# Wide attention in a four-layer transformer kernel: values issued in pairs every second tick, and the extras of a batch spread anew

## The chip, the cores and the metric

The kernel runs on one core of a Trainium2 chip. The metric is the device time of one execution in microseconds; the median of several runs is compared.

## The reference, cut to what matters

The model has four layers on a state x of 16 sequences of 256 positions and 128 channels. The change is in the attention of layers 0 and 1, the "wide" one: 16 heads of 64 channels. (h is the normed and modulated x.)

```python
# layer 0: causal, with normed and rotated q and k
q, k, v = split(h @ wqkv.T)            # 16 heads of 64
q, k = rope(rmsnorm(q, wq)), rope(rmsnorm(k, wk))
attn = softmax(where(causal, q @ k.T * 64 ** -0.5, -inf))
x = x + ga * ((attn @ v) @ wo.T)
# layer 1: a bias by relative position, no mask
scores = q @ k.T * 64 ** -0.5 + bias
x = x + ga * ((softmax(scores) @ v) @ o_w.T)
```

## The kernel before, in words

The whole program is one list of stages. Each engine runs them in the same order, and semaphores join the engines. `wide_attention` (line 414) makes two of the stages: the causal one (layer 0, some 40 to 660 us of the profile) and the biased one (layer 1, some 1050 to 1645 us).

**Ticks.** A batch is one of the 16 sequences. Its 16 heads make eight pairs, p = 8 b + j, and the stage's loop has one tick t per pair (lines 696, 870, 965, 1036). With u = t % 8, tick t also does 1/8 of the projections of a later batch a and prepares batch b = t // 8 + 1. What each engine does in a tick, and in which order, is written out by hand:

- TensorE (lines 696 to 709): `tensor_project`, in the causal stage `tensor_turn` (the rotated q and k transposed), `tensor_sums` (line 579, the transpose of the reciprocal sums, line 584), `tensor_extra` (line 586: V projection, output product c0 or c1, transposes of the norm), then scores of t, transposes of the probabilities of t-1 (line 643), and the value product of t-2 (`value`, line 653).
- VectorE (lines 870 to 887): copies or rotation products of the projection, `vector_spread` (copy of the turned sums, line 752), `vector_extra`, row maxima and their negation (`rowmax`, or `biased_rowmax`, line 809, with the negation in line 822), the reciprocal (line 762), the even half of the transposed probabilities of t-1 out of PSUM into TS (line 884), sums of squares.
- ScalarE (lines 965 to 984): copies, `scalar_extra`, the odd half of the transposed probabilities of t-1, the four exponentials of t (`exps`, line 934), and in odd ticks the copy of a finished pair of values from bank 4 into OT (line 982).
- GpSimd (`gpsimd_tick`, line 1002): in the causal stage K's scaling (line 1012), the rotation's additions (991, 992) and a power (1000); in both the scaling of OT by the reciprocal sums (line 1026) and the residual.
- SP: one round trip of the reciprocal sums through memory per batch (lines 1047 to 1058).

**Banks.** PSUM has eight banks. Pair p has banks 2 (p % 2) and the next for scores and, after the exponentials, for its transposes. So the scores of t+1 wait until both halves of the transposes of t-1 have been copied out (line 616), and VectorE makes its half after the maxima of t. Bank 4 takes the values of two pairs. Banks 5 to 7 are a ring: projection, q and k turned, V, sums' transpose, output product and norm transposes take its banks in turn, in the order of `take_tick` (line 495).

**Where the extras of a batch stand.** V's four parts at u = 2, 3, 4, 5 (`v_at`; parts 0 and 2 are copied by VectorE, 1 and 3 by ScalarE); the sums: reciprocal at u=0, transpose at 1, scalings at 3 and 4, output products at 6 and 7 (`posts`, line 472); the norm's transposes at 0, every second batch (`turned_in`, line 483).

**Buffers.** TS, the transposed probabilities, has two buffers. WM (768 columns) and CT hold the weights of the layer's modulation; WF has 6400 columns, of which the biased stage uses 6144.

## Time and profile before

| | us |
|---|---|
| median of 3 runs (2927.63 to 2938.03) | 2928.72 |
| profiled execution | 2927.48 |
| its span | 2924.9 |
| TensorE busy | 2768.8 (95%) |
| VectorE busy | 2120.6 (73%) |
| ScalarE busy | 1700.9 (58%) |
| GpSimd busy | 1043.8 (36%) |
| mean granted TensorE clock | 0.987 of full |

The span goes from the first to the last instruction; 2.6 us of the profiled execution's own time lie around it. Busy time is a union over an engine's instructions. A matmul's end is modelled, so starts are the better measure: the time from one set of probability transposes (line 643) to the next is a tick. One fp32 product is two records in the trace.

### The profile page before, as it was taken

To read this page: it belongs to the slowest core of one execution; us is meant where nothing else is said; L and a number is where in the kernel's file an instruction comes from. 1 tells how busy PE (TensorE), PEld (TensorE's weight loads), DVE (VectorE), ACT (ScalarE), POOL (GpSimd) and SP (SyncE) were. 2 spreads that over 40 slices of the span, in tenths; PEclk is the share of its full clock that TensorE was granted. 3 is DMA by queue.
4 is the path that set the end of the run, shared out by engine and by line. 5 is a ranking of instruction groups with operands and counts; after the bars stand their busy time and mean duration, and the time that the engine had idled before them with its cause. 6 is when DMAs were issued, how large, how long until landed. Compare 5 with 4: busy or idle time off the path is not lost.

```text
span 2924.9 us, 68989 instructions
## 1 busy us (share of the span) xinstructions
PE 2768.8 (95%) x25484; PEld 1867.5 (64%) x25484; DVE 2120.6 (73%) x5801; ACT 1700.9 (58%) x4109; POOL 1043.8 (36%) x1422
## 2 busy tenths in 40 slices
PE   5999999989999999999999799999989988999898
PEld 2666666666666666666666455567767765666676
DVE  6988888855666566666666699855678886887675
ACT  3888888873332367777776477644325544343665
POOL 6888888831000011111111345412243330104441
PEclk9999999999999999999999899999999999999999
DMA  3111111123000011111111554300026443245760
GB/s 106 23 24 31 31 31 31 31 74 102 1 15 1 1 36 31 31 31 30 24 26 28 144 158 131 102 1 16 1 80 174 124 120 79 59 103 131 192 178 26
DMA packets 191996, 186.96 MB, mean 64 GB/s; under 512 B 14528, under 2 KB 168192, under 8 KB 190896
## 3 DMA queue, kind: packets, MB, share of 16 engines
q1 hardware_dynamic: 191664, 182.56, 24.5%
q8 instruction: 205, 3.36, 0.5%
q14 instruction: 127, 1.04, 0.1%
HBM read 129.19 MB, written 53.31 MB: 62 GB/s over the span
## 4 chain that ended last, share of the span: by engine, by line
PE 75%; DVE 10%; ACT 6%; issue 3%; POOL 2%; DMA 2%; SPq 2%; ACTq 0%; DVEq 0%; POOLq 0%
PE pb L161 67%; ACT big L947 4%; PE pb L643 3%; ACT big L158 2%; DVE big L2198 2%; DVE big L817 1%; PE pb L576 1%; SPq L1869 1%; PE pb L2169 1%; DVE big L2699 1%; DMA big<-parts 1%; PE pb L246 1%; DVE big L233 1%; POOL big L1026 1%; DVE big L727 0%
## 5 line engine op out<-in xcount | busy, mean ns | idle before, releaser
L161 PE MATMUL pb<-big 64*128 64x256 bf16 (+12 forms) x20300 | 2509.7, 329 | 92.3 <-DVE big L2198 32.0
L161 PEld LDWEIGHTS pb<-big 128*128 128x128 f32 (+5 forms) x20300 | 1565.9, 145 | 834.6 <-issue 502.3
L158 ACT ACTIVATE big<-pb 128x512 f32<-128x512 f32 (+7 forms) x1444 | 828.5, 623 | 542.0 <-PE pb L161 308.1
L158 ACT ACTIVATE big<-pb,big 128x512 f32<-128x512 f32 (+2 forms) x536 | 316.0, 617 | 541.4 <-PE pb L161 476.8
L2198 DVE TENSOR_REDUCE big<-pb 128x4 f32<-128x1024 f32 (+1 forms) x256 | 277.6, 1086 | 75.6 <-PE pb L161 71.0
L172 POOL TENSOR_TENSOR big<-big 128x128 f32<-128x128 f32 x192 | 84.8, 456 | 649.3 <-DVE big L169 649.3
L947 ACT ACTIVATE big<-big 128x256 f32<-128x256 f32 x512 | 253.9, 498 | 69.8 <-DVE big L822 68.7
L947 ACT ACTIVATE big<-pb,big 128x128 f32<-128x128 f32 (+1 forms) x512 | 256.9, 525 | 61.1 <-DVE big L802 60.9
L817 DVE CUSTOM_DVE_ANT_0 big<-pb,big 128x256 f32<-128x256 f32 x512 | 186.6, 421 | 100.2 <-PE pb L161 100.2
L1543 DVE SCALAR_TENSOR_TENSOR big<-pb,big 128x128 f32<-128x128 f32 x512 | 144.0, 344 | 138.3 <-PE pb L161 137.5
L1026 POOL TENSOR_TENSOR big<-big 128x512 f32<-128x512 f32 x128 | 159.9, 1276 | 233.8 <-DMA big<-recip 233.7
L1521 DVE SCALAR_TENSOR_TENSOR big<-pb,big 128x512 f32<-128x512 f32 x200 | 148.5, 749 | 89.8 <-PE pb L161 60.6
L185 POOL TENSOR_SCALAR big<-big 128x4 f32<-128x4 f32 (+2 forms) x105 | 27.3, 260 | 495.2 <-DVE big L180 495.2
L643 PEld LDWEIGHTS pb<-big 64*128 64x128 f32 x3584 | 145.8, 139 | 74.9 <-ACT big L947 58.0
L643 PE MATMUL pb<-big 64*128 64x64 f32 x3584 | 158.0, 225 | 25.5 <-ACT big L947 24.6
L1000 POOL TENSOR_TENSOR big<-big 128x32 f32<-128x32 f32 x32 | 174.1, 5441 | 2.7
L727 DVE TENSOR_TENSOR big<-pb,big 128x512 f32<-128x512 f32 x256 | 163.7, 680 | 13.2 <-PE pb L161 11.4
L884 DVE COPY big<-pb 128x384 f32<-128x384 f32 (+1 forms) x256 | 156.8, 612 | 2.3 <-PE pb L643 2.1
L991 POOL TENSOR_TENSOR big<-big 128x256 f32<-128x256 f32 x128 | 83.7, 654 | 84.3 <-DVE big L727 81.1
L576 PEld LDWEIGHTS pb<-big 128*128 128x128 f32 x512 | 63.7, 142 | 75.9 <-issue 65.6
L947 ACT ACTIVATION_READ_ACCUMULATOR big<-pb,big 128x1 f32 x512 | 110.6, 216 | 0.0
L233 DVE TENSOR_SCALAR big<-big 128x128 f32<-128x128 f32 x256 | 97.5, 433 | 8.0 <-POOL big L187 7.9
(147 smaller groups left out, 2193.8 us busy)
## 6 DMA issues: line engine op xcount, KB each, us to landing
big<-parts SPq DMA_DIRECT2D x96, 512.0 KB, 4.2
parts<-big SPq DMA_DIRECT2D x384, 96.0 KB, 2.4
big<-recip SPq DMA_DIRECT2D x64, 512.0 KB, 6.6
big<-comb SPq DMA_DIRECT2D x32, 512.0 KB, 8.2
parts<-big SPq DMA_DIRECT2D x192, 64.0 KB, 2.1
big<-gates SPq DMA_DIRECT2D x7, 1024.0 KB, 6.1
big<-in_wf SPq DMA_DIRECT2D x1, 3072.0 KB, 14.7
big<-scratch SPq DMA_DIRECT2D x1, 3072.0 KB, 17.4
```

Of the source, the lines that this page charges most:

```text
L158: return e.activation(o, i, f, bias=bias, scale=scale)
L161: return e.matmul(o, l, r_, start=start, stop=stop, skip_group_check=True)
L643: t = e.transpose(banks[2 * (p % 2) + half][:, 64 * at:64 * at + 64], PS[p % 2][rows, i, 128 * blk:128 * blk + 128], IDF[rows, rows])
L727: t = e.tensor_tensor(h3(D), h3(bk), TAB[:, 2 * qk + kk, tile, :].unsqueeze(1).to_broadcast([128, 8, 64]), ALU.mult)
L817: t = e.tensor_tensor_reduce(ps[:, i, x], banks[2 * (p % 2) + i][:, x], U[:, 2 * j + i, 128 - 128 * qt:384 - 128 * qt], 1.0, -3.0e38, ALU. ...
L884: e.tensor_copy(*turned_out(t - 1, 0)).then_inc(even_out, 1)
L947: t = e.activation(ps, banks[2 * s + i][:, at:at + w] if causal else ps, ACT.Exp, bias=NM[s][:, m:m + 1], scale=rstd_q(b)[:, qt, h:h + 1] ...
L1000: e.tensor_tensor(half, half, HALF, ALU.pow).then_inc(rms_made, 1)
L1026: e.tensor_tensor(OT[k % 6], OT[k % 6], R[:, 2 * i:2 * i + 2, :], ALU.mult).then_inc(chunk_scaled, 1)
L1521: e.scalar_tensor_tensor(out=H[n % hn], in0=bk[:, :], scalar=B2[:, nf * u + f:nf * u + f + 1], in1=sg, op0=ALU.add, op1=ALU.mult).then_inc ...
L1543: x = e.scalar_tensor_tensor(out=ACC[s][:, i, :], in0=bk[:, 128 * i:128 * i + 128], scalar=CMB[s][:, E * i + u:E * i + u + 1], in1=ACC[s][ ...
L2198: e.tensor_reduce(m[:, :, 0:n, jj], two[:, :, 0:width].rearrange("p e (q x) -> p e q x", q=n), AXX, ALU.max, negate=True).then_inc(maxed, 1)
```

## The change

1. `value` is no longer called once a tick but twice in odd ticks, for pairs t-3 and t-2. The stage has 131 ticks in place of 130.
2. TS gets a third buffer: WM's columns in the causal stage, in the biased one 1024 columns made of WF's unused 256 and WM. The loads of the modulation's weights for layer 2 (CT and WM) move from the start of the biased stage to the narrow attention stage after it.
3. V's parts move to u = 3, 4, 5 and u = 0 of the batch after; the wait for V's copies goes from the scores of a batch's first pair to its first value. The sums' transpose moves from u=1 to 2, the scalings from 3 and 4 to 4 and 5, the norm's transposes from 0 to 1. Reciprocal (0) and output products (6, 7) stay.
4. In the biased stage the maxima are negated and announced per head of the pair, two negations of 2 columns in place of one of 4; `exps` goes head by head and waits for the second head's maxima only before its third exponential. In the causal stage the exponentials keep their order.
5. On GpSimd the scaling of OT comes first in its tick, ahead of K's scaling, additions, powers and norm.

```diff
@@ -111,6 +111,7 @@
         WF = alloc(6400)
+        spare_at = top[0] - 256
         WM = alloc(768)
@@ -435,7 +436,7 @@
             width = 384 if causal else 512
-            TS = [alloc(2 * width) for _ in range(2)]
+            TS = [alloc(2 * width) for _ in range(2)] + [WM if causal else big[:, spare_at:spare_at + 1024]]
             OT = [alloc(512).rearrange("p (j t) -> p j t", j=2) for _ in range(6)]
@@ -460,10 +461,15 @@
             hosted = not causal
-            last = 128 + 2
+            last = 128 + 3
             guests_at = 120 if causal else 112
             ahead = 2 if causal else 1
-            v_at = (2, 3, 4, 5)
+            def values_in(b, u):
+                found = (b - 1, 3) if u == 0 else (b, u - 3) if u in (3, 4, 5) else None
+                return [found] if found and 0 <= found[0] < 16 else []
@@ -471,7 +477,7 @@
-                return [(step, t // 8 - 1) for step, late in (("recip", 0), ("turn", 1), ("scale0", 3), ("scale1", 4), ("c0", 6), ("c1", 7))
+                return [(step, t // 8 - 1) for step, late in (("recip", 0), ("turn", 2), ("scale0", 4), ("scale1", 5), ("c0", 6), ("c1", 7))
                         if t >= 8 and t % 8 == late]
@@ -484,7 +490,7 @@
                     return (a + 1) // 2 if u == 7 else None
-                return (a + 1) // 2 if a < 15 and a % 2 == 1 and u == 0 else None
+                return (a + 1) // 2 if a < 15 and a % 2 == 1 and u == 1 else None
@@ -501,8 +507,8 @@
                         take(step, c, ring=ring)
-                if 0 <= b < 16 and u in v_at:
-                    take("v", b, v_at.index(u), ring=ring)
+                for v in values_in(b, u):
+                    take("v", *v, ring=ring)
                 for step, c in posts(t):
@@ -584,8 +590,8 @@
             def tensor_extra(e, t, a, b, u):
-                if 0 <= b < 16 and u in v_at:
-                    tensor_v(e, b, v_at.index(u))
+                for v in values_in(b, u):
+                    tensor_v(e, *v)
                 for step, c in posts(t):
@@ -609,7 +615,7 @@
                 if j == 0:
-                    for key in (("v", b, 2), ("v", b, 3)) + ((("turn", b, 7),) if causal else (("project", b, 6), ("project", b, 7))):
+                    for key in (("turn", b, 7),) if causal else (("project", b, 6), ("project", b, 7)):
                         s = slots[key]
@@ -647,11 +653,15 @@
                 n = width // 64
-                return (TS[p % 2].rearrange("p (n q) -> p n q", n=n)[:, :, 64 * half:64 * half + 64],
+                return (TS[p % 3].rearrange("p (n q) -> p n q", n=n)[:, :, 64 * half:64 * half + 64],
                         banks[2 * (p % 2) + half][:, 0:width].rearrange("p (n q) -> p n q", n=n))
...
                 b, j, c = p // 8, p % 8, p // 2
+                if j == 0:
+                    for n in (2, 3):
+                        s = slots["v", b, n]
+                        e.wait_ge(s.free, s.n)
                 e.wait_ge(even_out, p0 + p + 1)
@@ -661,7 +671,7 @@
                         t = mm(e, o[64 * i:64 * i + 64, 256 * (p % 2) + q0:256 * (p % 2) + 256], VB[b % 2][:, kb, 2 * j + i, :],
-                               TS[p % 2][:, width * i + 256 * kb:width * i + 256 * kb + 256 - q0], kb == 0, kb == 1)
+                               TS[p % 3][:, width * i + 256 * kb:width * i + 256 * kb + 256 - q0], kb == 0, kb == 1)
                 t.then_inc(pair_valued, 1)
@@ -703,7 +713,8 @@
                         turn(e, t - 1)
-                    if 0 <= t - 2 < 128:
+                    if t >= 3 and t % 2:
+                        value(e, t - 3)
                         value(e, t - 2)
@@ -770,8 +781,9 @@
                         residual_vector(e, r0 + qt, qt, bk[:, 0:128], 0).then_inc(s.free, 1)
-                if 0 <= b < 16 and u in v_at[0::2]:
-                    vector_v(e, b, v_at.index(u))
+                for v in values_in(b, u):
+                    if v[1] % 2 == 0:
+                        vector_v(e, *v)
                 c = normed_in(a)
@@ -816,14 +828,14 @@
                                                    U[:, 2 * j + i, 128 - 128 * qt:384 - 128 * qt], 1.0, -3.0e38, ALU.add, ALU.max,
-                                                   nm[:, 2 * qt + i:2 * qt + i + 1])
-                t.then_inc(own_v.sem, own_v.up())
-                e.wait_ge(own_v.sem, own_v.n)
-                e.tensor_scalar(nm, nm, -1.0, None, ALU.mult).then_inc(pair_maxed, 1)
+                                                   nm[:, 2 * i + qt:2 * i + qt + 1])
+                    t.then_inc(own_v.sem, own_v.up())
+                    e.wait_ge(own_v.sem, own_v.n)
+                    e.tensor_scalar(nm[:, 2 * i:2 * i + 2], nm[:, 2 * i:2 * i + 2], -1.0, None, ALU.mult).then_inc(pair_maxed, 1)
             def ts_writable(e, p):
-                if p >= 2:
-                    e.wait_ge(pair_valued, p0 + p - 1)
+                if p >= 3:
+                    e.wait_ge(pair_valued, p0 + p - 2)
@@ -885,6 +897,7 @@
                         guest.vector(e, t - guests_at)
+                e.wait_ge(pair_valued, p0 + 128)
@@ -920,8 +933,9 @@
             def scalar_extra(e, a, b, u):
-                if 0 <= b < 16 and u in v_at[1::2]:
-                    scalar_v(e, b, v_at.index(u))
+                for v in values_in(b, u):
+                    if v[1] % 2:
+                        scalar_v(e, *v)
                 c = turned_in(a, u)
@@ -932,21 +946,23 @@
             def exps(e, p):
                 s, b, j = p % 2, p // 8, p % 8
-                e.wait_ge(pair_maxed, p0 + p + 1)
+                e.wait_ge(pair_maxed, p0 + (p + 1 if causal else 2 * p + 1))
                 if p >= 2:
...
                     e.wait_ge(recip_made, b0 + b - 1)
-                for qt in range(2):
+                for n in range(4):
+                    qt, i = (n // 2, n % 2) if causal else (n % 2, n // 2)
                     at = 0 if qt == 0 else width - 256
                     w = 128 if causal and qt == 0 else 256
-                    for i in range(2):
-                        ps = PS[s][:, i, at:at + w]
-                        m, h = 2 * qt + i, 2 * j + i
-                        t = e.activation(ps, banks[2 * s + i][:, at:at + w] if causal else ps, ACT.Exp, bias=NM[s][:, m:m + 1],
-                                         scale=rstd_q(b)[:, qt, h:h + 1] if causal else 1.0,
-                                         accum_out=SM[b % 2][:, 2 * h + qt:2 * h + qt + 1])
+                    if n == 2 and not causal:
+                        e.wait_ge(pair_maxed, p0 + 2 * p + 2)
+                    ps, h = PS[s][:, i, at:at + w], 2 * j + i
+                    t = e.activation(ps, banks[2 * s + i][:, at:at + w] if causal else ps, ACT.Exp, bias=NM[s][:, n:n + 1],
+                                     scale=rstd_q(b)[:, qt, h:h + 1] if causal else 1.0,
+                                     accum_out=SM[b % 2][:, 2 * h + qt:2 * h + qt + 1])
                 t.then_inc(pair_exped, 1)
@@ -1000,6 +1016,14 @@
             def gpsimd_tick(e, t, a, b, u):
+                for step, c in posts(t):
+                    if step in ("scale0", "scale1"):
+                        half = int(step[5])
+                        e.wait_ge(ld_recip, 32 * (b0 + c + 1))
+                        for i in (2 * half, 2 * half + 1):
+                            k = 4 * c + i
+                            e.wait_ge(chunk_out, c0 + k + 1)
+                            e.tensor_tensor(OT[k % 6], OT[k % 6], R[:, 2 * i:2 * i + 2, :], ALU.mult).then_inc(chunk_scaled, 1)
                 if causal and 0 <= b < 16:
@@ -1017,14 +1041,7 @@
                 for step, c in posts(t):
-                    if step in ("scale0", "scale1"):
-                        half = int(step[5])
-                        e.wait_ge(ld_recip, 32 * (b0 + c + 1))
-                        for i in (2 * half, 2 * half + 1):
-                            k = 4 * c + i
-                            e.wait_ge(chunk_out, c0 + k + 1)
-                            e.tensor_tensor(OT[k % 6], OT[k % 6], R[:, 2 * i:2 * i + 2, :], ALU.mult).then_inc(chunk_scaled, 1)
-                    elif step in ("c0", "c1"):
+                    if step in ("c0", "c1"):
                         qt = 2 * c + int(step[1])
@@ -1042,8 +1059,6 @@
                     second_gates(e, 1)
-                    e.dma_start(CT, dr["c2"]).then_inc(ld_wm, 16)
-                    e.dma_start(WM, dr["wmod2"]).then_inc(ld_wm, 16)
                 for b in range(16):
@@ -1073,7 +1088,7 @@
                           lambda e, i: hosted_step(i, lambda *at: gpsimd_tick(e, *at)), nothing)
-            left = (3, 4, 6, 7)
+            left = (4, 5, 6, 7)
             tail = Guest(4, lambda i: take_tick(128 + left[i], 16, 17, left[i], ring=BK[6:8]),
@@ -2444,6 +2459,8 @@
                         e.dma_start(WA[:, 1152:2176], dr["rope8"]).then_inc(ld_wa, 16)
+                        e.dma_start(CT, dr["c2"]).then_inc(ld_wm, 16)
+                        e.dma_start(WM, dr["wmod2"]).then_inc(ld_wm, 16)
                     if k == 2 and b == 5:
```

## Rows read from the trace of the kernel before

**Rows 1.** Busy us of each engine (x instructions) by stretch, TensorE clock, DMA.

```profile
100.00:560.00 460.00, 453.79 (x4247) 299.02 (x4241) 403.66 (x822) 379.83 (x1164) 389.36 (x380) 1.00 0.15 31
1080.00:1535.00 455.00, 448.28 (x4017) 311.47 (x4015) 309.26 (x1207) 323.42 (x1058) 76.83 (x82) 1.00 0.15 30
```

**Rows 2.** Line 584 in those stretches, TensorE; first and last start.

```profile
L584 PE MATMUL pb<-big x13: 272/273/285, 101.8 to 553.2; 128*32 128x128 f32 x13
...
L584 PE MATMUL pb<-big x13: 272/272/273, 1081.0 to 1530.7; 128*32 128x128 f32 x13
```

**Rows 3.** Timeline, TensorE, biased stage; start, us, engine, line, what, count, idle.

```profile
1306.24 0.66 PE L643 MATMUL pb<-big 64*128 64x64 f32 x16
1306.83 4.07 PE L161 MATMUL pb<-big 128*64 128x256 f32 x22
1310.74 0.66 PE L643 MATMUL pb<-big 64*128 64x64 f32 x16
...
1325.53 5.00 PE L161 MATMUL pb<-big 128*64 128x256 f32 x36
```

**Rows 4.** Timeline, TensorE, narrow windows inside one tick of the biased stage.

```profile
1307.10 0.60 PE L161 MATMUL pb<-big 128*64 128x256 f32 x4
...
1307.32 0.39 PE L161 MATMUL pb<-big 128*64 128x256 f32 x2
...
1307.85 0.48 PE L161 MATMUL pb<-big 128*128 128x256 f32 x1
...
1308.82 0.59 PE L161 MATMUL pb<-big 128*128 128x512 f32 x1
...
1309.77 0.49 PE L161 MATMUL pb<-big 64*128 64x256 f32 x2
```

**Rows 5.** Timeline, TensorE, transposes of the first two biased ticks.

```profile
1049.59 0.71 PE L643 MATMUL pb<-big 64*128 64x64 f32 x16 [1.91 <-ACT big L947]
...
1053.13 0.66 PE L643 MATMUL pb<-big 64*128 64x64 f32 x16
```

**Rows 6.** Timeline, VectorE, biased stage, two ticks.

```profile
1303.89 0.35 DVE L762 RECIPROCAL big<-big 128x32 f32<-128x32 f32 x1
...
1306.46 0.42 DVE L817 CUSTOM_DVE_ANT_0 big<-pb,big 128x256 f32<-128x256 f32 x1 [0.24 <-PE pb L161]
...
1306.81 0.42 DVE L817 CUSTOM_DVE_ANT_0 big<-pb,big 128x256 f32<-128x256 f32 x1
...
1308.04 0.69 DVE L884 COPY big<-pb 128x512 f32<-128x512 f32 x1
```

**Rows 7.** Timeline, biased stage: sums' transpose, scalings, a negation.

```profile
1305.07 0.27 PE L584 MATMUL pb<-big 128*32 128x128 f32 x1
...
1315.69 4.97 POOL L1026 TENSOR_TENSOR big<-big 128x512 f32<-128x512 f32 x4 [12.20 <-DMA big<-recip]
...
1316.94 1.28 DVE L822 TENSOR_SCALAR big<-big 128x4 f32<-128x4 f32 x1
```

**Rows 8.** Timeline, TensorE, causal stage (PEld: its weight loads).

```profile
252.21 0.27 PE L584 MATMUL pb<-big 128*32 128x128 f32 x1
...
263.16 0.53 PE L643 MATMUL pb<-big 64*128 64x64 f32 x12
...
267.66 0.53 PE L643 MATMUL pb<-big 64*128 64x64 f32 x12
...
274.92 2.93 PE L161 MATMUL pb<-big 128*128 128x128 f32 x28
...
283.12 0.53 PE L643 MATMUL pb<-big 64*128 64x64 f32 x12
...
287.04 0.45 PEld L643 LDWEIGHTS pb<-big 64*128 64x128 f32 x12 [0.51 <-ACT big L947]
```

**Rows 9.** Timeline, GpSimd, causal stage.

```profile
263.88 2.51 POOL L1026 TENSOR_TENSOR big<-big 128x512 f32<-128x512 f32 x2
...
268.74 2.50 POOL L1026 TENSOR_TENSOR big<-big 128x512 f32<-128x512 f32 x2
```

## The prediction, made before the change was run

> **What bounds the kernel now.** The page comes first: its busy line and its slices show TensorE at nine tenths nearly everywhere, at a full clock, in the two stages that the diff touches. The busy time by stretch then sets those stages side by side [rows 1]: in the 460 us of the causal stage TensorE is busy 453.79 us, with VectorE at 403.66, GpSimd at 389.36 and ScalarE at 379.83 close behind; in the 455 us of the biased stage TensorE has 448.28 and VectorE only 309.26, GpSimd 76.83. So TensorE sets the pace, but in the causal stage three engines run little below it. The line of the sums' transpose, once a batch of eight ticks, gives the period [rows 2]: (553.2 - 101.8) / 12 = 37.62 us in the causal stage, (1530.7 - 1081.0) / 12 = 37.47 us in the biased one. Each stage has about 14 regular batches and two at its end.
>
> Next, one tick of the biased stage on TensorE, from the start of one set of probability transposes to the next: 1310.74 - 1306.24 = 4.50 us, no idle time [rows 3]. Its parts [rows 3, 4]: transposes 0.59, values 1.02 (1306.83 to 1307.85), projection 0.97, V projection 0.95, scores 0.97. A pass over two head halves takes 0.22 (1307.10 to 1307.32), so four passes of a value need 0.86 to 0.88 and the rest of the 1.02 is spent on entering and leaving that tile shape. The first ticks of the stage have no value yet and show what a tick without one costs [rows 5]: 1053.13 - 1049.59 = 3.54 us with V, 0.96 less. A causal tick with V and a value is 267.66 - 263.16 = 4.50 too [rows 8]; its second key block is half as wide, so I put its value at 0.96 - 0.22 = 0.74, and the second value of a pair at 0.65.
>
> Work of TensorE alone for a biased batch: eight ticks without V at 4.50 - 0.95 = 3.55, 28.4; four V, 3.8; two output products, each 5.00 - 4.07 + 0.95 = 1.88 above a plain tick [rows 3], 3.76; sums' transpose 0.2; norm transposes every second batch, 0.3. That is 36.4, so about 1.1 us of 37.47 is stall. In the causal batch V needs no change of tile shape, which I take as 0.1 less, 0.86; the rest is put alike: 8 x 3.64 + 4 x 0.86 + 3.6 + 0.4 = 36.6 of 37.62, 1.0 of stall.
>
> **Values in pairs.** A pair costs 0.96 + 0.86 = 1.82 in place of 2 x 0.96, so 0.10 less per two ticks, 0.4 per batch, in either stage. The third TS buffer makes this possible without a wait: at tick t the copy writes the buffer whose value was issued a tick earlier. What it does to the order matters more. An even tick now has no value: from scores of t to scores of t+1 TensorE has only transposes, projection, an extra and scores, 0.59 + 0.97 + 0.97 = 2.53 us plus the extra; the odd tick has 4.4 plus its extra. The extras sit at these places: even-to-odd intervals get norm transposes (u=1, half the batches), V (3), V (5), output product (7); the longer ones get V (0), sums (2), V (4), output product (6).
>
> **What is late next, biased stage.** Scores of t+1 need the bank that VectorE empties after it has finished the maxima of t. From the transposes' start at 1306.24 VectorE begins the maxima 0.22 later and reaches the copy at 1308.04, 1.80 later [rows 6]; the copy takes 0.69, end +2.49. The change negates each head's maxima by itself, in program order ahead of this copy. A maximum takes 1306.81 - 1306.46 = 0.35, so four of them leave 1308.04 - 1306.46 - 1.40 = 0.2 for wait and negation, and a second negation adds about as much: +2.70, with 0.05 for the semaphore (an estimate) +2.75. Then 0.97 of scores: an even-to-odd interval is at least 3.72 us. TensorE's own work for it is 2.55 without an extra, 2.85 as a mean over batches with and without a norm, 3.5 with V, 4.4 with an output product. Stalls: u=1, 3.72 + 0.27 (the reciprocal stands between negation and copy, 0.35 long, of which I put 0.27 as not overlapped) - 2.85 = 1.1; u=3, 0.2; u=5, 0.2; u=7 none. The exponentials are not this bound: with the first head's maxima ready two passes, 0.7 us, earlier they can start sooner. That part of the change is a gain on a chain that stops being last.
>
> **The negations and GpSimd.** In the tick of the trace where GpSimd begins its four scalings (1315.69, 4.97 us), VectorE's negation takes 1.28 us instead of 0.17, from 1316.94 to 1318.22, beside GpSimd's second one, which ends near it [rows 7]. The tick then waits for the exponentials. The change gives each tick two such negations and moves the scalings one tick later; they arrive 10.6 us after the sums' transpose (1315.69 against 1305.07), which lands in u=4, an even tick. First negation: 0.3 late; second: 0.5; so 0.75 more at u=5. Bounds: nothing if the scalings miss it, as much as 1.28 x 2 if both wait a whole scaling; I take 0.75. The Trainium skill (SBUF — State Buffer, section "SBUF: two separate sides") says of a port pair shared by VectorE and GpSimd that whoever starts first holds it for a whole instruction and the other fully blocks. The trace agrees with it, 1.28 against 0.17; were the long negation a chance of something else, the biased batch would come out 0.75 shorter, about 37.5.
>
> Biased sum: 36.4 - 0.4 + 1.1 + 0.2 + 0.2 + 0.75 = 38.25, against 37.47: +0.8 per batch, x14 = +11 us.
>
> **Causal stage.** Here the exponentials keep their order. With a long extra ahead of it, the interval 283.12 to 287.04 is 3.92 us and was ended by ScalarE [rows 8]: the chain scores, maxima, exponentials, transposes. Even-to-odd intervals of 2.9 + extra (3.76 with V) hit it at u=1 (stall 0.8), 3 and 5 (0.16 each). The present stalls of u=0 and 1 (3.92 against 3.64 at u=0, and at u=1 a tick made long by statistics or modulation) lie in the long intervals afterwards and go. Without more: 36.6 - 0.4 + 1.1 = 37.3, a gain of 0.3.
>
> Against it stands the moved sums' transpose. It goes from u=1 to u=2, the output product stays at u=6. Now: transpose 252.21, scalings from 263.88, last pair 268.74 to 271.24, product 274.92 [rows 8, 9]; the scalings end 19.0 after the transpose, 3.7 before the product, which is due 22.7 after it. The changed order takes out of this one interval of 4.5 and the stall of tick 1 (0.7 by the sum above), turns three of 4.5 into 3.92, 5.15 and 3.92 (-0.5) and adds a second value (+0.65): due at 17.65. The scalings will stand ahead of K's scaling and the additions of their tick, but a K scaling and an addition still lie between the two pairs, as now: 268.74 - 263.88 - 2.51 = 2.35, and 7.4 from first to end. The data land at +10.6 in the biased stage, where GpSimd waits for them idle [rows 7]; I put it at +10.85 here, with a slower copy ahead, so the end is at 10.85 + 7.4 = 18.25 and TensorE waits 0.6 us. Bounds: nothing if the data land by 10.25, 1.9 where one more GpSimd scaling's length (2.51 / 2) lies in the way. I take 0.85, nearer to the row. Causal sum: 37.3 + 0.85 = 38.15 against 37.62: +0.55, x14 = +8 us. In the biased stage GpSimd has nothing between the pairs, the scalings end at 15.6, 2 us before the product.
>
> **The ends and the loads.** In the last, emptier ticks the even ticks are stall-bound sooner: about +1 us per stage. The sums' transpose of the last batch goes behind two values in place of one, 0.7 to 1.0 us each time, on the chain that ends with the last scalings. Together +4. The two loads for the next modulation move into the narrow stage's SP queue: two issues among many, nothing on a chain, bounds 0 and 1.2.
>
> Sum: 11 + 8 + 4 = +23 on the profiled execution of 2927.5, so 2950.5; the median of the runs shown is 1.2 higher, 2951.7. I say 2951.
>
> **Rivals.** (1) No measurable change: the two tolls (0.75 at u=5, 0.85 at the causal product) are missed or halved. The batches are then 37.5 and 37.3 to 37.7, with the ends +4: 2928 to 2940. For it: each toll hangs on less than one us of alignment. Against: nothing removes the 3.72 of VectorE. (2) Faster: VectorE's copy doesn't gate the short intervals (its work slides into the long ones) and TensorE alone decides: 36.0 and 36.2 per batch, -1.45 x 28 = -41 us, 2888; the half of it, 2905 to 2910, if only the stalls that now stand at u=0, 1 and 4 go. For it: the biased stage has VectorE idle a third of the time. Against: the wait is one of order, not of load. (3) A dearer slow case: in the causal stage VectorE, at 88% busy, can't follow intervals of 3.9 with V on it at u=3 and 5, and comes late into the even tick: 0.6 more per causal batch and the whole second bound of the scalings, 1.05 more: x14 = 23, 2974. (4) That the change is empty can't be: the order of values differs in 126 ticks of each stage; it is part of (1).
>
> **Chances.** Forecast (2940 to 2963) 0.45; no change 0.26; faster 0.22; dearer 0.07. A measurement of this kernel can tell about 0.5%, 14.6 us, from no change; 2914 to 2943 is "same". Faster 0.22, same 0.27, slower 0.51. Range 2902 to 2968: it leaves out the best half of the faster case and the top of the dearer one. The forecast's own range is 2940 to 2963.
>
> **What would show it.** Right: transposes to transposes alternating about 3.7 to 3.9 and 5.3 us; idle time of TensorE ahead of scores in odd ticks, released by the VectorE copy (now hardly any); twice as many negations, some over 0.4 us, near the scalings; idle time before the first product of each causal batch, released by the GpSimd scaling; periods of the sums' transpose above 38. Wrong: a period below 37.3 in either stage, or short intervals of 3.5 with V and no idle time.

## The result, and the profile after

The changed kernel takes 2952.64 us (median of 4 runs, 2951.91 to 2956.15) against 2931.28 us for the kernel before (4 runs, 2927.63 to 2938.03): a ratio of 1.0075, 95% interval 1.0057 to 1.0093. It is slower by 21 us. Forecast were 2951 us and +23, with 2940 to 2963 as the forecast's own range. The profiled execution took 2951.91 us, its span is 2950.0, 25.1 above the span of before.

The busy line of the page: TensorE does the same 25484 matmuls and is busy for 25.5 us less. Of this 19.6 are the pairs' (2762.9 us are busy in the experiment e1 below, which differs in them alone); what makes up the rest was not taken apart.

```profile
PE 2743.3 (93%) x25484; PEld 1875.7 (64%) x25484; DVE 2129.2 (72%) x5929; ACT 1702.0 (58%) x4109; POOL 1042.0 (35%) x1422
```

The busy time by stretch of the changed kernel, to be read beside [rows 1]. In the same 455 us of the biased stage TensorE now has 3904 records, not 4017, and is busy 425.90 us, not 448.28: it waits 29.1 us in place of 6.7.

```profile
100.00:560.00 460.00, 442.26 (x4211) 297.95 (x4211) 393.76 (x817) 381.22 (x1155) 384.23 (x373) 1.00 0.15 29
1080.00:1535.00 455.00, 425.90 (x3904) 308.86 (x3902) 309.97 (x1277) 313.83 (x1035) 77.10 (x82) 1.00 0.14 30
```

The sums' transpose (now line 590) in the same stretches, once a batch. The periods are (524.1 - 106.3) / 11 = 37.98 us in the causal stage and (1514.2 - 1091.4) / 11 = 38.44 us in the biased one, against 37.62 and 37.47 [rows 2].

```profile
L590 PE MATMUL pb<-big x12: 272/273/273, 106.3 to 524.1; 128*32 128x128 f32 x12
...
L590 PE MATMUL pb<-big x12: 272/273/273, 1091.4 to 1514.2; 128*32 128x128 f32 x12
```

One biased batch on TensorE from the timeline (line 649 is the transposes of the probabilities, so the distance between two of its rows is a tick; the last bracket gives the idle time ahead of a row and what ended it):

```profile
1361.48 0.66 PE L649 MATMUL pb<-big 64*128 64x64 f32 x16
...
1364.21 1.14 PE L162 MATMUL pb<-big 64*128 64x256 f32 x8 [0.15 <-DVE big L896]
1365.18 0.66 PE L649 MATMUL pb<-big 64*128 64x64 f32 x16
...
1370.54 0.66 PE L649 MATMUL pb<-big 64*128 64x64 f32 x16
...
1374.38 1.14 PE L162 MATMUL pb<-big 64*128 64x256 f32 x8 [1.27 <-DVE big L896]
1375.35 0.66 PE L649 MATMUL pb<-big 64*128 64x64 f32 x16
...
1381.64 0.66 PE L649 MATMUL pb<-big 64*128 64x64 f32 x16
...
1386.04 0.66 PE L649 MATMUL pb<-big 64*128 64x64 f32 x16
...
1391.40 0.66 PE L649 MATMUL pb<-big 64*128 64x64 f32 x16
...
1394.34 1.13 PE L162 MATMUL pb<-big 64*128 64x256 f32 x8 [1.22 <-DVE big L896]
1395.31 0.66 PE L649 MATMUL pb<-big 64*128 64x64 f32 x16
```

Short and long ticks alternate: 3.70 (1361.48 to 1365.18), 5.36, 4.81, 6.29, 4.40, 5.36, 3.91. The short ticks with V (3.70 and 4.81) and the one of the reciprocal (3.91) have idle time in front of the scores, and each is ended by line 896, VectorE's copy. In the whole stretch TensorE's matmuls (PE) wait 29.0 us for this copy, which is nearly all of their 29.1 us of idle time. The weight loads (PEld) wait 52.8, but they overlap the matmuls, so the two rows are not to be added:

```profile
PEld pb L162 <- DVE big L896: 52.8, 36, 2.3
PE pb L162 <- DVE big L896: 29.0, 35, 1.5
```

In the kernel before, no matmul of this stretch waits for the copy (line 884 there). Some weight loads do, and the matmuls' idle time is ended by the exponentials:

```profile
PEld pb L161 <- DVE big L884: 15.6, 24, 1.0
...
PE pb L643 <- ACT big L947: 6.2, 20, 0.4
```

Why the third tick is 4.81 and not 3.7 can be read from GpSimd's and VectorE's timelines. GpSimd's four scalings:

```profile
1369.97 4.97 POOL L1026 TENSOR_TENSOR big<-big 128x512 f32<-128x512 f32 x4 [22.41 <-DMA big<-recip]
```

VectorE's two negations of that tick, the copy behind them, and one negation of the next tick for comparison:

```profile
1371.56 0.94 DVE L834 TENSOR_SCALAR big<-big 128x2 f32<-128x2 f32 x1
...
1373.22 0.52 DVE L834 TENSOR_SCALAR big<-big 128x2 f32<-128x2 f32 x1
1373.65 0.68 DVE L896 COPY big<-pb 128x512 f32<-128x512 f32 x1
...
1376.38 0.17 DVE L834 TENSOR_SCALAR big<-big 128x2 f32<-128x2 f32 x1
```

The first negation takes 0.94 us and ends at 1372.50, the second 0.52 and ends at 1373.74, both at the end of a scaling (four in 4.97 us: 1371.2, 1372.5, 1373.7); undisturbed it is 0.17. This is no single case: of the 256 negations of the stage 32 take more than 0.3 us, and 30 of these end within 0.03 us of the end of a scaling.

Mean time from transposes to transposes over 13 regular batches (second to fourteenth of each stage), from the starts of line 643 or 649, by the u of the tick at its end; the forecast's row is made of its own terms:

| | u=0 | 1 | 2 | 3 | 4 | 5 | 6 | 7 | sum |
|---|---|---|---|---|---|---|---|---|---|
| biased, before | 4.06 | 4.05 | 4.52 | 4.49 | 4.84 | 4.59 | 5.42 | 5.42 | 37.4 |
| biased, forecast | 5.35 | 3.99 | 4.61 | 3.72 | 5.35 | 4.47 | 6.28 | 4.46 | 38.2 |
| biased, after | 5.36 | 3.91 | 4.61 | 3.70 | 5.36 | 4.82 | 6.28 | 4.40 | 38.4 |
| causal, before | 4.00 | 4.43 | 4.56 | 4.51 | 4.52 | 4.65 | 5.49 | 5.43 | 37.6 |
| causal, forecast | 5.15 | 3.92 | 4.50 | 3.92 | 5.15 | 3.92 | 6.95 | 4.70 | 38.2 |
| causal, after | 5.16 | 3.67 | 4.47 | 4.27 | 5.16 | 4.26 | 6.26 | 4.63 | 37.9 |

The causal stage hides something of its own. GpSimd's scalings, VectorE's product of the maxima (line 814, a 128x4 tensor product in SBUF) beside them, and the projection of tick 5 in another batch:

```profile
192.76 2.50 POOL L1026 TENSOR_TENSOR big<-big 128x512 f32<-128x512 f32 x2 [4.40 <-DMA big<-recip]
...
197.43 2.53 POOL L1026 TENSOR_TENSOR big<-big 128x512 f32<-128x512 f32 x2
```

```profile
193.43 0.68 DVE L812 TENSOR_REDUCE big<-pb 128x2 f32<-128x512 f32 x1
194.14 1.14 DVE L814 TENSOR_TENSOR big<-big 128x4 f32<-128x4 f32 x1
```

```profile
230.77 0.53 PE L649 MATMUL pb<-big 64*128 64x64 f32 x12
231.75 1.13 PE L162 MATMUL pb<-big 128*128 128x512 f32 x2 [0.46 <-ACT big L159]
```

The product takes 1.14 us where it mostly takes 0.16, and ends when a scaling does. And the projection starts 0.98 after the transposes, where it starts 0.46 after them in a tick without such a wait (235.46 after 235.00). ScalarE ended that wait; in the code it is ScalarE's square that frees the ring bank which the projection takes. Over the 13 regular batches the projection of tick 3 waits so in every one, 0.5 us on average, that of tick 5 in three. Neither was in the forecast. What was in it, matmuls of the product at u=6 waiting for GpSimd's scalings, comes to little in the 460 us:

```profile
PE pb L162 <- POOL big L1026: 0.4, 2, 0.2
```

### The profile page after: what moved, and what is told of

It reads as the page before. It is cut to its first block, busy times and chain, and to the rows that moved or that the text cites. A ratio compares the mean times of both kernels' runs of the same rounds, so it can differ in the third digit from the quotient of the medians.

```text
span 2950.0 us, 69113 instructions
## 1 busy us (share of the span) xinstructions
PE 2743.3 (93%) x25484; PEld 1875.7 (64%) x25484; DVE 2129.2 (72%) x5929; ACT 1702.0 (58%) x4109; POOL 1042.0 (35%) x1422
## 3 DMA queue, kind: packets, MB, share of 16 engines
q14 instruction: 128, 1.05, 0.1%
## 4 chain that ended last, share of the span: by engine, by line
PE 70%; DVE 13%; issue 5%; ACT 4%; POOL 4%; DMA 2%; SPq 1%; DVEq 0%; ACTq 0%; POOLq 0%
PE pb L162 64%; DVE big L829 2%; ACT big L963 2%; PE pb L649 2%; ACT big L159 2%; DVE big L2213 2%; SPq L1884 1%; POOL big L1026 1%; DVE big L896 1%; PE pb L2184 1%; DVE big L738 1%; DVE big L2716 1%; PE pb L582 1%; DVE big L812 1%; POOL big L1016 1%
## 5 line engine op out<-in xcount | busy, mean ns | idle before, releaser
L162 PE MATMUL pb<-big 128*128 128x128 f32 (+12 forms) x20300 | 2491.0, 329 | 151.5 <-DVE big L896 51.2
L829 DVE CUSTOM_DVE_ANT_0 big<-pb,big 128x256 f32<-128x256 f32 x512 | 196.0, 421 | 134.5 <-PE pb L162 134.4
L963 ACT ACTIVATION_READ_ACCUMULATOR big<-pb,big 128x1 f32 x512 | 103.5, 202 | 0.0
L234 DVE TENSOR_SCALAR big<-big 128x128 f32<-128x128 f32 x256 | 91.5, 411 | 8.4 <-POOL big L188 8.2
```

The source lines that it names most:

```text
L162: return e.matmul(o, l, r_, start=start, stop=stop, skip_group_check=True)
L829: t = e.tensor_tensor_reduce(ps[:, i, x], banks[2 * (p % 2) + i][:, x], U[:, 2 * j + i, 128 - 128 * qt:384 - 128 * qt], 1.0, -3.0e38, ALU. ...
L963: t = e.activation(ps, banks[2 * s + i][:, at:at + w] if causal else ps, ACT.Exp, bias=NM[s][:, n:n + 1], scale=rstd_q(b)[:, qt, h:h + 1] ...
```

## The experiments

All of them keep the whole computation but one (short scalings). In the cuts of code, `...` stands for lines left out. Times are medians against runs of the kernel before on the same chip, with the 95% interval of the ratio; periods come from the sums' transpose, as above.

**One value a tick** (e1_each_tick), the pairs alone undone.

```diff
-                    if t >= 3 and t % 2:
-                        value(e, t - 3)
+                    if 0 <= t - 2 < 128:
                         value(e, t - 2)
```

> The changed kernel, but one value a tick as before; places of the extras, third buffer and split negation kept. Theory (short even ticks are what costs): no interval is held at 3.7 any more, ticks are 4.5 with V; biased period about 37.4 or less (36.4 of TensorE + 0.3 at u=1 + 0.7 where GpSimd holds the negations) against 38.44, causal about 37.3 against 37.98; total 2925 to 2935. Rival (the new places of the extras cost, not the pairs): stays at 2950.

Measured: 2927.19 us, 0.9981 (0.9970 to 0.9992).

```profile
L590 PE MATMUL pb<-big x13: 272/273/273, 105.7 to 553.7; 128*32 128x128 f32 x13
...
L590 PE MATMUL pb<-big x13: 272/273/273, 1084.5 to 1528.0; 128*32 128x128 f32 x13
```

Periods (553.7 - 105.7) / 12 = 37.33 and (1528.0 - 1084.5) / 12 = 36.96. Time and periods are as expected or below. The pairs cost 25 us (2952.64 against 2927.19); everything else in the change together is a small gain, 5 us. TensorE's waits for VectorE's copy in the biased stretch fall from 29.0 to 5.7 us. The rival falls.

**Pairs, extras at their old places** (e5_old_places).

```diff
-                found = (b - 1, 3) if u == 0 else (b, u - 3) if u in (3, 4, 5) else None
+                found = (b, u - 2) if u in (2, 3, 4, 5) else None
...
-(("recip", 0), ("turn", 2), ("scale0", 4), ("scale1", 5), ("c0", 6), ("c1", 7))
+(("recip", 0), ("turn", 1), ("scale0", 3), ("scale1", 4), ("c0", 6), ("c1", 7))
...
-                return (a + 1) // 2 if a < 15 and a % 2 == 1 and u == 1 else None
+                return (a + 1) // 2 if a < 15 and a % 2 == 1 and u == 0 else None
...
-            left = (4, 5, 6, 7)
+            left = (3, 4, 6, 7)
```

> The changed kernel with pairs, but the extras back where they were (V at 2 to 5, sums' transpose 1, scalings 3 and 4, norm's transposes 0). Theory: the 3.7 floors stay (u=1, 3, 5), but the scalings fall into the long tick after u=3, so their toll of 1.1 at u=5 goes: biased period 37.5, causal 37.5; total 2933. Rival (the pairs are the whole cost): 2950.

Measured: 2931.89 us, 1.0001 (0.9992 to 1.0011).

```profile
L590 PE MATMUL pb<-big x13: 272/273/285, 101.7 to 555.9; 128*32 128x128 f32 x13
...
L590 PE MATMUL pb<-big x13: 284/285/286, 1079.7 to 1530.2; 128*32 128x128 f32 x13
```

Periods (555.9 - 101.7) / 12 = 37.85 and (1530.2 - 1079.7) / 12 = 37.54. The biased ticks u=1, 3 and 7 stay at 3.91, 3.70 and 4.40, and u=5 comes down to 3.80, as the toll leaves it. As expected, but for the causal stage, which stays at 37.85 and not 37.5. So 20 us hang on where the extras meet the pairs: a batch of short and long ticks has a parity, and the change had put the scalings on the short side. That it is the scalings shows in the regular batches of the biased stage, 0.9 us or 13 us in all: u=5 falls by 1.02 there, while V's and the norm's moves nearly cancel (u=0 5.36 to 4.70, u=2 4.61 to 5.36). In the causal stage the regular batches give 2 us. The rest lies in the last batches of the stages and was not taken apart.

**A single negation** (e3_one_negation); `exps` waits for it once.

```diff
-                    t.then_inc(own_v.sem, own_v.up())
-                    e.wait_ge(own_v.sem, own_v.n)
-                    e.tensor_scalar(nm[:, 2 * i:2 * i + 2], nm[:, 2 * i:2 * i + 2], -1.0, None, ALU.mult).then_inc(pair_maxed, 1)
+                t.then_inc(own_v.sem, own_v.up())
+                e.wait_ge(own_v.sem, own_v.n)
+                e.tensor_scalar(nm, nm, -1.0, None, ALU.mult).then_inc(pair_maxed, 1)
...
-                e.wait_ge(pair_maxed, p0 + (p + 1 if causal else 2 * p + 1))
+                e.wait_ge(pair_maxed, p0 + p + 1)
...
-                    if n == 2 and not causal:
-                        e.wait_ge(pair_maxed, p0 + 2 * p + 2)
```

> The changed kernel with a single negation and one announcement per pair of heads in the biased stage. Theory: the exponentials, 4.05 after the scores, take the place of VectorE's 3.72 as the floor of the even-to-odd intervals: +0.35 at u=3, +0.15 at u=1, about the same at u=5: biased period 38.9 to 39.1, total 2960. Rival (the second negation is itself the toll): period under 38.2, total 2948 or less.

Measured: 2961.94 us, 1.0105 (1.0086 to 1.0125).

```profile
L590 PE MATMUL pb<-big x12: 272/272/273, 1096.4 to 1523.3; 128*32 128x128 f32 x12
```

The period is (1523.3 - 1096.4) / 11 = 38.81, and u=1 and u=3 are both 4.05 us. The time is as expected, the period a little under. The chain of the exponentials is the floor again; the split negation is worth 9 us within the changed kernel. At u=5 the single negation is cheaper, 4.61 against 4.82, so the rival's toll exists but is the smaller part.

**Short scalings** (e4_short_scalings). GpSimd scales 8 of 256 columns; the others stay unscaled, so this kernel's result is not the model's, and only its times count.

```diff
-                            e.tensor_tensor(OT[k % 6], OT[k % 6], R[:, 2 * i:2 * i + 2, :], ALU.mult).then_inc(chunk_scaled, 1)
+                            e.tensor_tensor(OT[k % 6][:, :, 0:8], OT[k % 6][:, :, 0:8], R[:, 2 * i:2 * i + 2, 0:8], ALU.mult).then_inc(chunk_scaled, 1)
```

> The changed kernel with GpSimd's scalings cut to 8 of 256 columns (the rest of OT is left unscaled), in both stages. Theory: negations and products of the maxima are no longer held behind a GpSimd scaling; biased u=5 falls from 4.82 to 3.70 us, causal u=5 from 4.26 to about 3.75: periods 37.3 and 37.5, total 2930. Rival (u=5 is long because of VectorE's own work): u=5 stays above 4.6 in the biased stage, total 2950.

Measured: 2915.67 us, 0.9948 (0.9934 to 0.9962).

```profile
L590 PE MATMUL pb<-big x13: 272/273/273, 106.0 to 555.3; 128*32 128x128 f32 x13
...
L590 PE MATMUL pb<-big x12: 272/273/273, 1113.1 to 1524.4; 128*32 128x128 f32 x12
```

Periods (555.3 - 106.0) / 12 = 37.44 and (1524.4 - 1113.1) / 11 = 37.39. Biased u=5 falls to 3.75, causal u=5 to 3.91 and u=6 to 6.13. The toll in the biased stage is 1.05 us a batch. The time is 37 us under the changed kernel's, 14 more than expected. Of the 38.5 us between the two profiled executions, 14 batches at 1.05 and 0.54 give 22. What I had not counted: the last batches of the two stages give 4; the stretch from the causal stage's last transposes to the biased stage's first is 6 shorter, since the last four scalings, 5 us long, stand in the chain that ends the causal stage; and the stretch behind the biased stage, whose code is the same, was 7 us shorter in this profiled execution.

**The split alone, on the kernel before** (e2_before_split). Its edit is the reverse of e3's together with the changed `exps`.

> The kernel before with one part of the change alone: maxima negated per head and exponentials head by head in the biased stage. Theory: the chain scores to exponentials of 4.05 falls to about 3.4, so u=0 falls to 3.7 and the sums' tick stays near 4; the second negation can be held by GpSimd too, which adds up to 0.5 at u=4. Biased period 36.9 to 37.1 against 37.47, causal unchanged, total 2922 to 2926. Rival (the split only adds an instruction): 2932 or more.

Measured: 2921.91 us, 0.9965 (0.9951 to 0.9979).

```profile
L584 PE MATMUL pb<-big x13: 272/273/273, 1081.7 to 1523.3; 128*32 128x128 f32 x13
```

The period is (1523.3 - 1081.7) / 12 = 36.80, a little better than expected, and the causal one is 37.62 as before. By itself this part of the change is a gain of 9 us. e1, which keeps all of the change but the pairs, gained 5, so the other parts together gained nothing that these runs show.

**ScalarE negates** (e6_pairs_scalar, e7_each_tick_scalar, e9_old_places_scalar). VectorE announces each head's maxima at once; ScalarE makes the negation ahead of that head's exponentials, 0.19 us of work (the cut shows the edit of `exps` alone). e7 puts this on e1, e9 on the old places with one value a tick.

```diff
+                    if n % 2 == 0 and not causal:
+                        if n:
+                            e.wait_ge(pair_maxed, p0 + 2 * p + 2)
+                        e.activation(NM[s][:, n:n + 2], NM[s][:, n:n + 2], ACT.Copy, scale=-1.0).then_inc(own_a.sem, own_a.up())
+                        e.wait_ge(own_a.sem, own_a.n)
```

> The changed kernel, with the negation of the biased stage made by ScalarE ahead of each head's exponentials, none on VectorE. Theory: VectorE's floor falls to 2.3 + 0.97 = 3.3 and no negation can be held by GpSimd; the exponentials take over at about 3.85, so u=1, 3 and 5 come to 3.85: biased period 37.5 to 37.6 against 38.44, total 2940. Rival (u=5 is held by something other than the negation): u=5 stays near 4.8, total 2950.

Measured: 2944.29 us, 1.0048 (1.0031 to 1.0064).

```profile
L591 PE MATMUL pb<-big x12: 272/272/273, 1096.8 to 1511.6; 128*32 128x128 f32 x12
```

The period is (1511.6 - 1096.8) / 11 = 37.71 and the total 4 us over what was expected; u=1, 3 and 5 are 3.84, 3.85 and 3.84, as expected. With no negation on VectorE nothing is held at u=5. Three floors in the same place have now been read: 3.70 by VectorE's copy, 3.85 and 4.05 by the exponentials.

> One value a tick, the changed places, the negation on ScalarE. Theory: u=5 of the biased stage falls from 4.88 to 4.49 and u=1 stays at or under 3.98: biased period 36.5 against 36.96, total 2921. Rival (ScalarE, now with the longer chain, holds short ticks at 3.85 to 4.1): 2927 as without it.

Measured: 2921.59 us, 0.9972 (0.9961 to 0.9982).

```profile
L591 PE MATMUL pb<-big x13: 272/272/273, 105.5 to 555.8; 128*32 128x128 f32 x13
...
L591 PE MATMUL pb<-big x13: 272/273/273, 1087.1 to 1527.4; 128*32 128x128 f32 x13
```

Periods (555.8 - 105.5) / 12 = 37.53 and (1527.4 - 1087.1) / 12 = 36.69; u=5 of the biased stage is 4.49. Total and u=5 are as expected, the period 0.2 over.

> One value a tick, the extras where they were before, third buffer, scalings first in GpSimd's tick, the negation on ScalarE. Theory: the causal product no longer waits for the scalings (5.84 to 5.49 at u=6), but statistics and norm make u=1 long again as before (4.5): causal period 37.4 to 37.6; biased 36.5. Total 2920 to 2925. Rival (the new places are the better ones): more than e7_each_tick_scalar by 5.

Measured: 2927.59 us, 0.9998 (0.9988 to 1.0008).

```profile
L591 PE MATMUL pb<-big x13: 272/273/273, 102.1 to 557.9; 128*32 128x128 f32 x13
...
L591 PE MATMUL pb<-big x13: 272/273/273, 1085.7 to 1530.9; 128*32 128x128 f32 x13
```

A miss, and its rival holds: periods (557.9 - 102.1) / 12 = 37.98 and (1530.9 - 1085.7) / 12 = 37.10, 6 us slower than e7. So without pairs, and with the rest as in e7, the new places are the better ones. It shows at u=1 (biased 3.95 against 4.26, causal 3.97 against 4.44) and at the causal u=5 (4.53 against 4.96). My reading for u=1, that the norm's modulation and the statistics no longer fall on the same tick's chain, is argued from the order and not shown. Nor does it hold for old places as such: e2, with the old places and GpSimd's old order, takes 2921.91 us, as little as e7.

**Scalings at their old place in GpSimd's tick** (e8_scalings_last): the block of the scalings moved back behind K's scaling and the additions.

> The changed kernel with GpSimd's scalings at their old place in its tick, behind K's scaling and the additions. Theory: in the causal stage the first pair starts later only by what GpSimd has not finished when the data land, and the second pair no earlier; the product at u=6 waits up to 1 us more, or a hold at u=5 moves by as much; the biased stage has nothing else on GpSimd and stays at 38.44. Total 2950 to 2965. Rival (scalings first only delay K's scaling): faster, 2945 or less.

Measured: 2955.01 us, 1.0092 (1.0076 to 1.0108).

```profile
L590 PE MATMUL pb<-big x12: 272/273/273, 108.9 to 530.5; 128*32 128x128 f32 x12
```

Within what was expected. The causal period is (530.5 - 108.9) / 11 = 38.33 against 37.98; u=5 is 4.11, but u=6 waits until 6.81 in every batch. The biased stage stays at 38.46. The times alone, 2955.01 and 2952.64 with overlapping intervals, don't tell the two apart; by the causal period the move is a small gain at these places. At the old places no run tests it alone.

**Both scalings in one tick** (e10_scalings_together), on e7.

```diff
-(("recip", 0), ("turn", 2), ("scale0", 4), ("scale1", 5), ("c0", 6), ("c1", 7))
+(("recip", 0), ("turn", 2), ("scale0", 4), ("scale1", 4), ("c0", 6), ("c1", 7))
```

> As e7_each_tick_scalar, with both pairs of scalings in tick 4, K's scaling and additions behind them. Theory: in the causal stage the scalings end 2.4 earlier, so the product at u=6 does not wait (5.94 falls to 5.49) and one product of maxima less is held: causal period 37.0 against 37.53, biased unchanged at 36.7, total 2914 to 2917, under both kernels. Rival (K's scaling, late by 2.4, holds the turned k at u=6 or 7): no gain.

Measured: 2910.61 us, 0.9942 (0.9928 to 0.9956), the fastest of all, under both kernels.

```profile
L591 PE MATMUL pb<-big x13: 272/273/273, 105.4 to 547.7; 128*32 128x128 f32 x13
...
L591 PE MATMUL pb<-big x12: 272/272/273, 1116.2 to 1519.7; 128*32 128x128 f32 x12
```

The causal period is (547.7 - 105.4) / 12 = 36.86; u=6 falls from 5.94 to 5.46, as expected. The second effect, a product of the maxima less held, isn't seen: u=5 is 4.53 and 4.52. The total is 3 us better than the expected range, which no run explains.

**ScalarE's copy of a pair of values later** (e11_late_copy).

```diff
-                    if 0 <= t - 2 < 128 and t % 2 == 1:
-                        c = (t - 2) // 2
-                        e.wait_ge(pair_valued, p0 + t - 1)
+                    if 0 <= t - 3 < 128 and t % 2 == 0:
+                        c = (t - 3) // 2
+                        e.wait_ge(pair_valued, p0 + t - 2)
```

> The changed kernel, but ScalarE copies a finished pair of values out of bank 4 at the end of the even tick instead of the odd one, half a microsecond of work off the way to its squares. Theory (in the causal stage the projection of an odd tick waits for the ring bank that ScalarE's square of the even tick frees): causal u=3 falls from 4.48 to 3.9 or 4.0 where it is long, u=5 falls by up to 0.4, u=1 stays at 3.6 to 3.8: causal period 37.3 to 37.5 against 37.98; the biased stage stays at 38.4; total 2943 to 2948. Rival (these ticks are long by VectorE's work): causal period 37.9 to 38.1, total 2952.

Measured: 2949.08 us, 1.0075 (1.0051 to 1.0100).

```profile
L590 PE MATMUL pb<-big x12: 272/273/273, 107.0 to 524.6; 128*32 128x128 f32 x12
```

The waits view of the causal stretch, the changed kernel first, then this one:

```profile
PE pb L162 <- ACT big L159: 7.7, 15, 0.7
...
PE pb L162 <- ACT big L159: 3.6, 12, 0.4
```

A miss: the period is the rival's. The ticks moved the way of the theory, if by less (u=3 from 4.27 to 4.09, u=5 from 4.26 to 4.11), but the causal period is (524.6 - 107.0) / 11 = 37.96, unchanged: what they gave, u=2 (4.47 to 4.62) and u=6 (6.26 to 6.43) took. In those of its batches whose u=5 is short, 3.70 to 3.76, u=6 is 6.6; where it is long, 4.4 to 4.7, u=6 is 6.2. The product's wait for the scalings stands behind whatever wait comes before it. That the bank's wait alone makes u=3 long is thus supported, not settled.

## Why the prediction was right, point by point

- **TensorE alone sets the pace before.** Right. With one value a tick the biased period reaches 36.96 (e1) and 36.69 (e7), near the 36.4 that was summed for TensorE's own work, and the causal one 36.86 (e10), near its 36.6.
- **A pair saves 0.10.** Right in kind, short in size. The unhindered long ticks are 5.36 and 5.16, forecast 5.35 and 5.15, but the short one with the output product is 4.40 and not 4.46. Two ticks with a product took 5.42 + 5.42 before and take 6.28 + 4.40 now, 0.16 less. Over 128 pairs this is 20 us, which is what TensorE's busy time gained (19.6 against e1). The forecast had taken a single value as 0.96, from the stage's first ticks, and not as the 1.02 of its own rows.
- **VectorE's copy behind two negations is the floor, 3.72 us.** Right, 3.70, and 3.91 with the reciprocal (3.99). It is idle time ahead of the scores, ended by line 896. Without negations on VectorE (e6) the exponentials' 3.85 stands in its place; without short ticks (e1) the waits fall from 29.0 to 5.7 us. The point was one of order: VectorE is busy 309.97 of 455 us and still ends these waits.
- **The chain of the exponentials becomes harmless.** Right; without the split it is 4.05 (e3).
- **The toll of the scalings at u=5, 0.75.** The mechanism was right, the size short: 1.1 (4.82 against 3.70, and e4's 3.75). The two negations were put at 0.3 and 0.5 late; in the row they are 0.77 and 0.35. The scalings come 9.66 after the sums' transpose (1369.97 against the 1360.31 of line 590), not 10.6: VectorE, idle here, copies the sums 0.3 after the transpose, not 0.9. The rule of the Trainium skill that the prediction draws on (SBUF — State Buffer, section "SBUF: two separate sides") stood the test: both negations end with a scaling, in this tick and in the other regular batches.
- **The causal stage, +0.55 a batch.** 0.36 by the period, and that it came so near is luck. The largest term, 0.85 for TensorE's wait for the scalings at u=6, failed: that wait is 0.13 as a mean (6.26 against e4's 6.13) and stands in 3 of 13 batches, at 0.4 to 0.5. The scalings end 17.6 to 18.1 after the sums' transpose, forecast 18.25; and the product, forecast due at 17.65, comes later, since u=3 and u=5 are each 0.35 longer than the 3.92 of the forecast. At u=3 it is the wait for the ring bank, at u=5 mostly the product of maxima that GpSimd holds, with the exponentials behind it (e4: 4.26 to 3.91). e8, with later scalings, has the wait at u=6 in every batch. The floor at u=1 was 3.67, not 3.92.
- **The rivals.** None held: no change and faster wanted periods under 37.7, measured are 37.98 and 38.44; the dearer case wanted 38.15 + 1.65 = 39.8 in the causal stage. But what the third one feared, short intervals of the causal stage that its engines can't follow, is there in part (u=3 and u=5).
- **The ends.** From the first to the last transposes of a stage the causal one is 6.1 us longer and the biased one 15.3, forecast 9 and 12. The other 3.7 of the span lie outside: 4.8 more behind the biased stage, 0.3 more between the two, 1.4 less ahead of the first. Over the profiled executions of all kernels here the stretch behind the biased stage spreads over 10 us, so it is not read.

The total of 2951 against 2952.64 is closer than its terms, and so far luck: the biased stage was forecast 3 us too small, the causal one 3 too large.

## What to carry to other kernels

When work is taken out of every second step, ask at once what else stands between two steps: here three of the four short steps of a biased batch ran into the next wait in the order of another engine, though that engine had a third of its time free. A batch of uneven steps has a parity, and everything with a due time of its own (a round trip through memory, a helper on a shared port) must be placed against it; moving the extras here by one step was worth 20 us. And when several waits lie one behind the other, removing the first shows the next: measure the period, not the tick.

## What was not expected of the hardware

A tensor product over only 128x4 elements in SBUF on VectorE was held for 1.14 us, against 0.16 undisturbed, until a GpSimd scaling ended. The Trainium skill (SBUF — State Buffer, section "SBUF: two separate sides") says that a VectorE operation with two SBUF inputs contends for the shared port pair with a GpSimd operation that reads SBUF, and that the second to start is blocked until the first is done. The trace agrees, 1.14 us against 0.16. The negation of the biased stage, held for up to 1.14 us on VectorE, on ScalarE (e6) took 0.19 us in every one of 256 cases (0.186 to 0.204) beside the same scalings.
